# Attention denominators: inverses laid out as 16 heads by 8 token blocks, spread to the channels by transfers instead of matmuls

## The reference

```
xq = clip(q / 4), xk = clip(k / 4);  Tq, Tk = Chebyshev polynomials 0..10 of xq, xk
kv_prefix = cumsum_s(Tk * v)                     # per channel and order
ks_prefix = cumsum_s(Tk.sum(channels of a head)) # per head and order
num = sum_n Tq * beta_n * kv_prefix              # per channel
den = sum_n Tq.sum(channels) * beta_n * ks_prefix  # per head: one number for 16 channels
out_h = num / (den[..., None] + 1e-7);  attention = out @ W_out.T
x = x + ga * attention;  then layernorm, router (top 2 of 8 experts), shared + routed SiLU experts, x = x + gb * ffn
```

## Time and profile before

| | |
|---|---|
| median of 3 runs | 1037.01 us |
| the profiled execution | 1036.65 us, of which the span of instructions is 1034.9 us |
| PE busy | 935.0 us, 90% of the span |
| DVE busy | 890.0 us, 86% |
| ACT busy | 475.8 us, 46% |
| POOL busy | 399.9 us, 39% |
| granted TensorE clock, mean | 0.971 of full speed |
| DMA traffic | 59.34 MB |

### The profile page before, as it was taken

How to read it: one execution, slowest core, us unless ns; L and a number is a source line. 1 busy time by engine, 2 the same in 40 slices (tenths; PEclk the granted TensorE clock), 3 DMA queues, 4 the chain that set the end, 5 groups by cost and what they waited for, 6 DMA issues and landing times. The chain is left out here.

```text
span 1034.9 us, 15465 instructions
## 1 busy us (share of the span) xinstructions
PE 935.0 (90%) x4889; PEld 674.1 (65%) x4889; DVE 890.0 (86%) x1385; ACT 475.8 (46%) x702; POOL 399.9 (39%) x631
## 2 busy tenths in 40 slices
PE   3965659999999999999999999999999999989995
PEld 3643346685767676776857676776758676757774
DVE  2488989999999999999999999999999999998431
ACT  4343345553536455554635454455535364431431
POOL 2022454443625244443625253443535152443210
PEclk9977889999999999999999999999999999999998
DMA  8103222223323132223332231232332231312111
GB/s 283 47 1 61 61 41 64 49 63 61 71 45 79 21 63 70 41 61 61 72 61 61 40 69 44 41 73 49 72 61 41 41 72 22 67 36 46 42 21 20
DMA packets 38428, 59.34 MB, mean 57 GB/s; under 512 B 2067, under 2 KB 31198, under 8 KB 38374
## 3 DMA queue, kind: packets, MB, share of 16 engines
q0 software_dynamic: 15360, 33.56, 19.0%
q1 hardware_dynamic: 21410, 22.72, 6.7%
q10 hardware_dynamic: 1604, 2.46, 0.7%
HBM read 16.77 MB, written 16.79 MB: 32 GB/s over the span
## 5 line engine op out<-in xcount | busy, mean ns | idle before, releaser
L797 ACT ACTIVATE hid<-ring,b1row 128x512 f32<-128x512 f32 x144 | 98.6, 685 | 177.5 <-PE ring L1279 177.5
L639 POOL DMA_DIRECT2D feat<-feat x48 | 45.7, 952 | 334.3 <-DVE feat L984 150.3
L1416 PE MATMUL acc<-w,hid 128*128 128x256 f32 x640 | 156.4, 391 | 0.0
L1416 PEld LDWEIGHTS acc<-w,hid 128*128 128x128 f32 x640 | 115.3, 189 | 30.0 <-issue 14.5
L1111 DVE TENSOR_TENSOR hid<-hid,cfb 128x512 f32<-128x512 f32 x128 | 86.3, 674 | 41.8 <-PE cfb L1390 41.1
L752 ACT ACTIVATE feat<-ring,bqkv 128x512 f32<-128x512 f32 x96 | 66.1, 689 | 109.0 <-PE ring L1279 109.0
L963 DVE TENSOR_TENSOR_SCAN feat<-zero,carry,feat 128x512 f32<-128x512 f32 x80 | 111.8, 1446 | 0.0
L963 DVE TENSOR_TENSOR_SCAN feat<-zero,feat 128x512 f32<-128x512 f32 x80 | 108.5, 1403 | 0.0
L1279 PE MATMUL ring<-n2H,w1H 128*128 128x512 f32 x288 | 99.9, 428 | 0.0
L1279 PE MATMUL ring<-n2H,w1L 128*128 128x512 f32 x288 | 91.0, 397 | 0.0
L1279 PE MATMUL ring<-n2L,w1H 128*128 128x512 f32 x288 | 90.6, 395 | 0.0
(11 more groups left out here) (167 smaller groups left out, 2013.9 us busy)
## 6 DMA issues: line engine op xcount, KB each, us to landing
feat<-feat POOLq DMA_DIRECT2D x48, 512.0 KB, 4.6
xin<-in_L_attn_x SPq DMA_DIRECT2D x16, 512.0 KB, 5.4
out<-x SPq DMA_DIRECT2D x16, 512.0 KB, 4.5
out<-fin POOLq DMA_DIRECT2D x16, 512.0 KB, 6.1
gates<-gate_rows SPq DMA_DIRECT2D x16, 128.0 KB, 4.7
feat<-in_L_wmod SPq DMA_DIRECT2D x1, 1536.0 KB, 14.1
feat<-in_L_attn_W_in SPq DMA_DIRECT2D x1, 768.0 KB, 9.5
const<-in_constants ACTq DMA_DIRECT2D x1, 690.5 KB, 4.1
```

Source lines behind the costliest of these rows:

```text
L639: g.dma_start(f(into), f(of), accum_op=ALU.add).then_inc(added[n], 16)
L797: a.activation(hid[:, e % NG], ring[bank][:, :], ACT.Silu, bias=b1row[:, e:e + 1]).then_inc(ring_copied, 1)
L1416: last = mm(acc[t // 2][:, t % 2], x[:, t * P:(t + 1) * P], w[:, e // 2], start=False, stop=(e == E), skip_group_check=True)
```

## The change

The inverse denominators get another layout, and the spread another carrier.

- `densum` is now 8 matrices of 128 x 128. Matmul b (L1355 in the changed kernel) puts the 16 denominators of token block b (64 tokens) on partitions h * 8 + b; the 8 matmuls accumulate into `misc[:, 0:64]`. So head h and block b share a partition, and a row of the tile holds 64 tokens. There were 4 matmuls before.
- `invert` works on 128 x 64 elements, before on 128 x 128.
- SP stores the reciprocals, 32 KB, to a scratch tensor in memory, `inv_rows`, of 16 rows by 512 tokens. It waits for that store, and for `added[0]`, then issues two loads. Load k reads 8 rows, each 16 times over, into the 128 partitions of `attn[:, k]`: 256 KB each.
- `divide` waits for both loads, and multiplies `feat[:, W, k]` by `attn[:, k]` in place.
- The 8 selection matmuls on PE and their constants (`headsel`) are gone.
- SP's loop over batch rows is written out, with waits on constants.

```diff
@@ constants
-CONSTS = {"ident": P, "headsum": 4 * QS, "densum": QS, "headsel": NT * KD * P, "kshift": 1, "rowmask": 2,
+CONSTS = {"ident": P, "headsum": 4 * QS, "densum": NB * P, "kshift": 1, "rowmask": 2,
...
-            for copy in range(QS // H):
-                c["densum"][row, copy * H + half * HPH + h] = w
+            for b in range(NB):
+                c["densum"][row, b * P + (half * HPH + h) * NB + b] = w
@@ SP
+            def spread_inverse(i, p):
+
+                c = number(i, p)
+                sp.wait_ge(den_inv, c + 1)
+                sp.dma_start(inv_rows.rearrange("h (b t) -> (h b) t", b=NB), denom[:, 1]).then_inc(inv_written, 16)
+                sp.wait_ge(added[0], 16 * (c + 1))
+                sp.wait_ge(inv_written, 16 * (c + 1))
+                for k in range(KD):
+                    rows = inv_rows[k * HPH:(k + 1) * HPH].unsqueeze(1).to_broadcast([HPH, DH, CT])
+                    sp.dma_start(attn[:, k], rows).then_inc(inv_spread, 16)
...
                 if loads or i < B:
+                    spread_inverse(i, p)
                     store_x1(i, p)
...
-            with sp.Fori(2, B - 2) as i:
+            for i in range(2, B - 2):
@@ DVE
-                v.tensor_scalar(denom[:, 0], misc[:, 0:P], EPS_DEN, None, ALU.add).then_inc(den_eps, 1)
+                v.tensor_scalar(denom[:, 0], misc[:, 0:TB], EPS_DEN, None, ALU.add).then_inc(den_eps, 1)
...
                 dve.wait_ge(numerator, c + 1)
+                dve.wait_ge(inv_spread, 32 * (c + 1))
                 for k in range(KD):
-                    dve.wait_ge(inv_spread, 2 * c + k + 1)
-                    v.tensor_tensor(attn[:, k], feat[:, W, k], tr[k][:, :], ALU.mult).then_inc(attn_ready, 1)
+                    v.tensor_tensor(attn[:, k], feat[:, W, k], attn[:, k], ALU.mult).then_inc(attn_ready, 1)
@@ PE
-                for t in range(NT):
-                    last = mm(misc[t * QS:(t + 1) * QS, 0:P], cv["densum"],
-                              prod[:, t * P:(t + 1) * P], start=True, stop=True)
+                for b in range(NB):
+                    last = mm(misc[:, 0:TB], cv["densum"][:, b * P:(b + 1) * P],
+                              prod[:, b * TB:(b + 1) * TB], start=(b == 0), stop=(b == NB - 1))
...
-            def spread_inverse(i, p):
...
                 expert(5)
-                if attn_:
-                    spread_inverse(i, p)
                 expert(6)
```

More of the change, by code:

```diff
@@ L27 @@
 LQ = 2 * QS
+NB = P // H
+TB = CT // NB
 XS = 4
@@ L71, in constants @@
             w = GAMMA[n] if n in (0, 2, 4) else 1.0
-            for copy in range(QS // H):
-                c["densum"][row, copy * H + half * HPH + h] = w
+            for b in range(NB):
+                c["densum"][row, b * P + (half * HPH + h) * NB + b] = w
             c["kshift"][row, 0] = {1: -0.5 * DH, 3: -0.125 * DH}.get(n, 0.0)
-    for q in range(4):
-        for half in range(KD):
-            c["headsel"][q * QS + half * HPH + ch // DH, (q * KD + half) * P + ch] = 1.0
     c["rowmask"][:SPL // 2, 0] = 1.0
@@ L131, in build @@
         gate_rows = nc.dram_tensor("gate_rows", [B, 2 * D], f32).ap()
+        inv_rows = nc.dram_tensor("inv_rows", [H, CT], f32).ap()
         bqkv = sb("bqkv", [P, 6, B])
@@ L155, in build @@
         kcarry = sb("kcarry", [P, 1])
-        denom = sb("denom", [P, 2, P])
+        denom = sb("denom", [P, 2, TB])
         logT = sb("logT", [P, CT])
@@ L247, in build @@
         den_ready, den_eps, den_inv = sem("denominators"), sem("denominators_eps"), sem("denominators_inverse")
-        inv_spread = sem("inverse_spread")
+        inv_written, inv_spread = sem("inverse_written"), sem("inverse_spread")
         attn_ready = sem("attention_ready")
```

## The result

| | before | after |
|---|---|---|
| median time | 1037.26 us | 1046.33 us |
| fastest and slowest run | 1036.67 to 1038.57 | 1046.19 to 1046.76 |
| span of the profiled execution | 1034.9 us | 1044.5 us |
| mean granted TensorE clock | 0.971 | 0.945 |

The ratio is 1.0087, with a 95% interval of 1.0074 to 1.01. The forecast was faster, 1033.4 us. The time lies in the range given, but the sign is wrong.

What follows compares the result with a forecast made beforehand. The bound was taken as a loop of a 21.7 us DVE leg and a 36.0 us PE leg. Terms -6.1 (chunks 2 to 14), -0.3, +2.0 and +0.8 sum to -3.6 us: 1033.4 us, faster, range 1029.5 to 1048.

Steps and rivals of the forecast that it cites:

- The DVE leg: DVE's 21.7 us stretch up to expert 8's weighting; the narrower inversion shortens it by 0.47 us a step, counted in full.
- PE's selection products buy nothing: Before expert 6 on PE, the freed 2.7 us buy nothing beyond DVE's 0.47 us and turn into waiting.
- The clock falls: Rival: after about 1.5 us idle before expert 6, TensorE gets 1.2 GHz; 24 us lost, 1057 us, chance 0.02.
- The chain of transfers: Between invert and divide, store plus two loads take 6.9 us (bounds 5.4 and 8.6), hidden within 7.8 us.
- the upper bound of 5.2: Longest time forecast for the two loads, in us from the start of the first; 4.8 was taken.
- Chunk 0, +2.0: In chunk 0, with no experts to hide the transfers, the division comes 2.0 us late.
- Chunk 1, +0.8: In chunk 1 the transfers land at 148.1 against 147.29, so 0.8 us late.
- Chunk 15, -0.3: In chunk 15 on PE, 1.78 us of selection products go and 1.45 us of sums come: 0.3 us gained.

Runs made afterwards that it cites:

- run 1: The changed kernel plus 8 unread matmuls between experts 5 and 6 in every step with experts: 1039.34 us, ratio 1.0028.
- run 4: The kernel before without its selection products and the waits for them, dividing by what stands in tr: 1054.14 us, ratio 1.0157.
- run 3: The changed kernel without its store and two loads, so the division reads old values: 1043.66 us, ratio 1.007.
- run 5: The kernel before with addition and reciprocal on only 64 of the 128 columns: 1031.6 us, ratio 0.9949.
- run 2: The changed kernel plus three unread matmuls between experts 5 and 6 in the steps with experts: 1041.24 us, ratio 1.0038.
- run 8: The changed kernel with the wide layout and selection products of the kernel before in chunks 0, 1, 14 and 15, no unread matmuls: 1041.64 us, ratio 1.0052.

## Why the prediction was wrong

- *The DVE leg, 0.47 us a step:* right. 683.75 and 683.90 us from chunk 2 to 14 where the clock stays up, against 689.53: 0.47 to 0.48 a step.
- *PE's selection products buy nothing; they "turn into waiting":* right as far as it goes, and here lies the failed step. The waiting was costed at nothing. The wait came out at 1.63 to 1.95 us in chunks 2 to 13, in the place and with the releaser named (about 1.5 was forecast), and in most steps the clock fell behind it. Runs 1 and 4 show the cost from both sides: 9.6 us by the trace in 12 steps.
- *The rival "The clock falls", chance 0.02:* this was the case, at a smaller price. It was dismissed because PE had waited 1.10 and 0.68 us within 4 us at full speed. That evidence speaks of two short waits, not of one long one; the runs show the difference between them. Its price of 24 us took every step and a whole projection at the low level. In fact 8 steps in 12 fall, at some 1.2 us each (9.6 / 8): the low clock covers the rest of expert 6 and a part of experts 7 and 8, and the projection runs in its 3.6 us.
- *The chain of transfers, 6.9 us, hidden with 0.9 to spare:* right in the middle. The division never waits there. The Trainium skill's rule (DMA: Bandwidth & Descriptors, "Why a DMA increments its semaphore by 16 and not by 1") gave 8 engines for the loads; the trace agrees in so far as the share of busy DMA engines is 0.52 and 0.53 in the two microseconds from 494.5 to 496.5, in which chunk 7's loads move, about half. In chunk 1, where it does wait, it starts 6.6 us after the store's issue, 5.1 after that of the first load. In chunk 0 it starts 5.5 us after the first load's issue, just past the upper bound of 5.2.
- *Chunk 0, +2.0:* +4.1. The store took 3.8 us, not 1.8, behind GpSimd's accumulating transfer, which the prediction had not looked for on this chunk. It held that no other transfer runs in that stretch; the trace before has this one at 89.63, 0.8 us after the start of chunk 0's reciprocal. And 1.3 us more came from the projection at the low clock. Run 3 shows the 4.4 us to be the transfers'.
- *Chunk 1, +0.8:* +0.9, near it by luck. The division's wait for the loads is 1.10 us, but the stretch is 0.9 us longer without the transfers as well (run 3). In the changed kernel the projection starts 0.7 us later behind the reciprocal than before (8.58 against 7.87) and takes 5.68 us instead of 5.38; in run 3 it starts 0.35 us earlier than before (7.52) and takes 6.71. So here too the clock costs what the sum left out: 0.3 us with the transfers, 1.3 without.
- *Chunk 15, -0.3:* the last two stretches give +0.8. The sums, 2.00 us, stand ahead of the up-projection there and are followed by matmuls at the low clock; no run isolates this, so it isn't shown. In run 5, with the old sums and no transfers, these two stretches are 1.0 us longer than before (148.49 against 147.53), so a difference of this size comes without either.

## What to carry to other kernels

Work taken off an engine that is not the bound can cost time, if it opens one long gap on TensorE: read the granted clock by stretch before and after, and price every gap that a change makes or lengthens. Where the removed work was itself what kept the clock up, replace it by unread matmuls only in the gaps that exist; where there is none, as in chunk 14, they are paid in full. And price the first and last chunks by themselves: in chunks 0 and 1 nothing hid the round trip through memory.

## What the runs showed of the hardware that was not expected

- The clock fell behind some single waits of 1.6 to 1.8 us and not behind others of the same length. In the changed kernel, waits of 1.65, 1.68 and 1.70 us before expert 6 were followed by it, and 1.63 (twice), 1.67 and 1.76 were not; all five from 1.93 to 1.95 were. Waits of 0.94 to 1.27 us at the same place never were in run 2. The length alone doesn't decide: in run 8 waits of 1.58 and 1.59 us were followed by it and one of 1.67 was not, and in run 4 one of 2.35 us, in chunk 2, was not. What else decides is open.
- The fall comes late. In chunk 7 it shows 0.6 us after PE had resumed work, which is why the row of the wait itself looks harmless and the matmuls behind it must be read.
- A store of 32 KB in rows of 256 bytes landed in 1.4 us in the median, in 3.8 us when an accumulating transfer of 512 KB had been issued 1.1 us ahead of it, and in 2.6 and 2.4 us when that was 2.2 and 3.5 us ahead.
